# A recurrence of eight small networks on one core: the matrix passes, waits and instruction orders of all four engines rearranged

## Chip, cores and metric

The kernel runs on one core of one Trainium2 chip. The metric is the device time of one execution in microseconds (us). The kernel before took 5656.33 us, the median of three runs that lie between 5656.32 and 5656.89.

## What is computed

2048 sequences are advanced through 256 time steps. One step of one sequence, cut to what matters:

```python
encoded   = tanh(xt @ We + st @ Ue + be)                     # 24 numbers
new_state = tanh(einsum(xt, Wx) + einsum(st, Ws) + bk)       # 8 candidates of 32
inp = concatenate([encoded, err])                            # the newest of 20 remembered entries
mem = concatenate([inp, mem[:-1]])
a        = relu(mem.reshape(-1) @ enc_w1 + enc_b1)           # 500 numbers -> 64
agent_in = relu(a @ enc_w2 + enc_b2)                         # 16
h1, c1 = lstm(agent_in, h1, c1);  h2, c2 = lstm(h1, h2, c2)
gate  = softmax(h2 @ gate_w + gate_b)                        # 8
theta = clamp01(mean(abs(mem[:10, -1])) * 2.5)
gate  = gate * theta + gs * (1 - theta)
st    = sum over the 8 candidates of gate * new_state        # 32
pred  = clamp01(st[-1]);  err = pred - yt
```

Nothing of a step can be computed for good before the step ahead of it has given `st`, but for the part of `a` that comes from the 19 older entries.

## The kernel before

The sequences are split into two groups of 1024 (g = 0 and 1). One group at one step is an *item*; items are numbered n = 1, 2, ..., with the groups alternating, so item n+2 is the next step of the group of item n. There are 512 items. In what follows X is an item, Y the next one (the other group), W the one ahead of X, so the state that W leaves is what Y starts from.

Every engine executes a list of instructions written out by hand, `run_phases` (L158): once per item it calls the engine's own `phase(items, extra)` with three items in flight, `new`, `cur` and `old`, each one younger than the next. Five steps, ten phases, form one trip of a hardware loop. The engines run freely and meet only at semaphores: `wait_ge(q, n)` ahead of an instruction, `.then_inc(q, 1)` at its end. So what sets the order of the work is, on each engine, the order of the calls in `phase`, and between engines those waits. One execution of the four phase lists for one item is called a *turn* below. The length of a turn, times 512, is nearly the whole time.

**TensorE (PE), L280 to L476.** In the order of the list: `encoded_s` (L311, the state's part of the encoder input), `logit_bias` (L417) and `gate_logits` (L424) for the softmax, `encoder1_now` (L368, the newest entry's part of `a`), `encoder2` (L379), `bias_of_cell` (L390) and `cell_gates` (L402) once for each LSTM cell, `candidates_x` and `candidates_s` (L322, L338) for the eight candidate states, `encoded_x` (L300), `state_transpose` (L285). The older entries' part of `a` is `history` (L357): four blocks, each of three passes (high and low fp16 halves of weights and entries), each pass two matmuls of 512 columns that use one half of the array's columns each and run side by side. Blocks 0 and 1 of an item run a turn ahead of blocks 2 and 3. They depend on nothing recent and fill the places at which TensorE would wait.

**ScalarE (ACT), L478 to L600.** `state_take` (L495, the transposed state to SBUF), `at_least_zero` and `encoded` (L507, L500), `entry_high` (L513), `encoder1` (L520), `agent_input` (L526), `cell_tanhs` and `value_tanh` (L545, L551) of each cell, `next_hidden` (L557), the candidates' tanh in four quarters (`candidates`, L535), `exponentials` (L565).

**VectorE (DVE), L602 to L834.** `cell_terms` (L691), `cell_value` (L697) and `new_hidden` (L703) of each cell; `errors` (L682); the softmax and gate in eight small instructions (`peaks` L721, `below_peak` L726, `totals`, `reciprocals`, `shares` L742, `fresh_gate` L747, `new_gate` L753), whose result goes to PSUM; the product of candidates and gate (`mix`, L760: pair 1 whole, of pair 0 one half) and four sums over the candidates (`mix_sum`, L780, each one half hf of one pair), which give the state; `prediction` (L788).

**GpSimd (POOL), L836 to L930.** `mix_quarter` (L864, the other half of pair 0), `new_error` (L893), `keep_prediction` (L903), `kept_share` and `kept_gate` (L843, L849: the part of the gate that is kept), `entry_low` (L876, the low half of the entry) and `gate_in_sbuf` (L857). `new_gate` on VectorE waits for `kept_gate`.

**SyncE (SP), L193 to L278**, loads inputs and weights ahead and writes each entry to the ring `hist` with four DMAs once `entry_low` and `encoder1_now` of it are done; `history` of the group's next step waits for them.

The four lists before (TensorE L441, ScalarE L570, VectorE L799, GpSimd L915) are in the listing and on the removed side of the diff.

## Time and profile before

| | |
|---|---|
| median of 3 runs | 5656.33 us |
| span of the profiled execution | 5654.1 us |
| instructions | 184300 |
| TensorE busy | 5444.6 us, 96% |
| VectorE busy | 4678.1 us, 83% |
| ScalarE busy | 3830.9 us, 68% |
| GpSimd busy | 1646.7 us, 29% |
| DMA | 172.38 MB, 30 GB/s |
| mean granted TensorE clock | 0.998 of full |

A busy share counts the time in which an engine had an instruction under way. A matmul's end is modelled, so TensorE counts as busy while a matmul drains and nothing new streams. PEld is TensorE's weight load. In a timeline a row merges neighbouring instructions of one line: the first number is the start, the second the time from the first one's start to the last one's end, x how many; in brackets the engine's idle time before it and what ended it. L numbers are lines of the kernel before.

### The profile page before, as it was taken

The page shows a single profiled execution, that of the slowest core. Times are in us where ns is not written, and L with a number is a line of the kernel's source. Part 1 is how long each engine was busy: PE and PEld are TensorE (multiplying, and loading weights), DVE is VectorE, ACT ScalarE, POOL GpSimd, SP SyncE. Part 2 cuts the span into 40 slices and gives each one's busy share as a digit, 9 for nine tenths or more (in the row PEclk, how much of TensorE's full clock was granted, in tenths as well). Part 3 has the DMA queues.
Part 4 walks back from the last instruction along what each step waited for, and adds up shares of the span by engine and source line. Part 5 has one row for each costly group of instructions (what it writes and reads, how often), then busy time and mean ns, then how long its engine had stood idle before and what let it go on. Part 6 is the DMA issues. An engine that isn't in the chain of part 4 may idle for free.

```text
span 5654.1 us, 184300 instructions
## 1 busy us (share of the span) xinstructions
PE 5444.6 (96%) x67584; PEld 3397.7 (60%) x67584; DVE 4678.1 (83%) x12841; ACT 3830.9 (68%) x9217; POOL 1646.7 (29%) x3589
## 2 busy tenths in 40 slices
PE   7999999999999999999999999999999999999998
PEld 4666666666666666666666666666666666666665
DVE  7888888888888888888888888888888888888887
...
GB/s 66 28 29 30 28 31 28 31 28 31 28 31 28 31 28 28 31 28 31 28 31 28 31 28 31 28 29 30 28 31 28 31 28 31 28 31 28 31 28 39
DMA packets 299286, 172.38 MB, mean 30 GB/s; under 512 B 156734, under 2 KB 263882, under 8 KB 298714
## 3 DMA queue, kind: packets, MB, share of 16 engines
...
q14 instruction: 8, 0.07, 0.0%
...
## 4 chain that ended last, share of the span: by engine, by line
PE 69%; ACT 15%; DVE 12%; issue 4%; DMA 0%; POOL 0%; ACTq 0%; POOLq 0%; DVEq 0%
PE chain L412 17%; PE a_ps L374 10%; PE cand_ps L343 8%; PE cand_ps L334 8%; ACT a_sb L523 6%; PE chain L399 6%; PE a_ps L363 6%; ACT gates L548 5%; DVE cell_in L708 5%; DVE added L694 4%; PE chain L308 4%; PE a_ps L385 4%; PE chain L429 4%; PE cand_ps L329 3%; ACT tanh_c L554 3%
## 5 line engine op out<-in xcount | busy, mean ns | idle before, releaser
L363 PE MATMUL a_ps<-hist,w_hist 125*64 125x512 f16 x12288 | 1700.2, 381 | 24.9 <-DMA w_hist<-enc_table 24.9
L785 DVE TENSOR_REDUCE state<-mixed 128x64 f32<-128x512 f32 x2048 | 1352.6, 681 | 34.1 <-POOL mixed L873 0.7
L541 ACT ACTIVATE cand<-cand_ps 128x512 f32<-128x512 f32 x2048 | 1154.6, 590 | 184.8 <-PE cand_ps L343 184.8
L412 PE MATMUL chain<-cell_in,cell_w 128*64 128x128 f32 x16384 | 1092.8, 276 | 0.7 <-ACT cell_in L531 0.5
L412 PEld LDWEIGHTS chain<-cell_in,cell_w 128*64 128x64 f32 x16384 | 888.3, 136 | 288.2 <-ACT cell_in L531 181.5
L900 POOL TENSOR_TENSOR err_ring<-pred_now,ys 128x8 f32 x512 | 128.6, 251 | 3106.0 <-DVE pred_now L792 3106.0
L548 ACT ACTIVATE gates<-chain 128x512 f32<-128x512 f32 x1024 | 611.4, 597 | 619.8 <-PE chain L412 619.8
L363 PEld LDWEIGHTS a_ps<-hist,w_hist 125*64 125x64 f16 x12288 | 658.6, 110 | 447.2 <-issue 26.0
L554 ACT ACTIVATE tanh_c<-gates 128x128 f32<-128x128 f32 x1024 | 316.7, 309 | 690.0 <-DVE gates L700 690.0
L694 DVE SCALAR_TENSOR_TENSOR added<-gates 128x256 f32<-128x256 f32 x1024 | 435.5, 425 | 419.4 <-ACT gates L548 419.4
L708 DVE SCALAR_TENSOR_TENSOR cell_in<-gates,tanh_c 64x128 f32<-64x128 f32 x2048 | 588.0, 287 | 159.4 <-ACT tanh_c L554 145.6
L873 POOL TENSOR_TENSOR mixed<-cand,gate 128x512 f32<-128x512 f32 x512 | 653.8, 1277 | 119.3 <-POOL gate L861 119.1
L769 DVE TENSOR_TENSOR mixed<-cand,chain 128x1024 f32<-128x1024 f32 x512 | 624.9, 1220 | 17.8
L374 PE MATMUL a_ps<-entry,w_now 100*64 100x256 f32 x4096 | 555.0, 388 | 61.2 <-ACT entry L504 0.4
L334 PE MATMUL cand_ps<-w_x,x_sb 32*128 32x256 f32 x8192 | 528.6, 374 | 0.0
L343 PE MATMUL cand_ps<-w_s,state_t 32*128 32x256 f32 x8192 | 528.6, 374 | 0.0
L523 ACT ACTIVATE a_sb<-a_ps,columns 128x512 f32<-128x512 f32 x512 | 351.7, 687 | 201.8 <-PE a_ps L374 201.8
L343 PEld LDWEIGHTS cand_ps<-w_s,state_t 32*128 32x128 f32 x8192 | 401.2, 185 | 40.9
L334 PEld LDWEIGHTS cand_ps<-w_x,x_sb 32*128 32x128 f32 x8192 | 403.8, 185 | 29.3
L399 PE MATMUL chain<-indicator,cell_bias 128*64 128x512 f16 x2048 | 416.1, 403 | 0.0
L531 ACT ACTIVATE cell_in<-a_ps,columns 64x128 f32<-64x128 f32 x1024 | 371.2, 362 | 37.6 <-PE a_ps L385 0.5
L374 PEld LDWEIGHTS a_ps<-entry,w_now 100*64 100x64 f32 x4096 | 293.0, 136 | 147.9 <-issue 102.8
...
## 6 DMA issues: line engine op xcount, KB each, us to landing
...
hist<-entry_parts SPq DMA_DIRECT2D x2048, 25.0 KB
...
```

Of the source, the lines that this page charges most:

```text
L334: nc.tensor.matmul(cand_ps[q][:, NS * hf:NS * hf + NS], x_sb[rows, x_slot(u), g, P * hf:P * hf + P], w_x[rows, :], start=False, stop=False ...
L343: last = nc.tensor.matmul(cand_ps[q][:, NS * hf:NS * hf + NS], state_t[rows, g, P * hf:P * hf + P], w_s[rows, :], start=False, stop=True, ...
L363: nc.tensor.matmul(a_ps[g][ENC * half:ENC * half + ENC, :], w_hist[0:HROWS, w_slot(u), kk, wp, :], hist[0:HROWS, xp, k, at:at + 512], star ...
L374: last = nc.tensor.matmul(a_ps[g][rows, COLS * p:COLS * p + COLS], w_now[0:ER, p, rows], entry[0:ER, g, :], start=False, stop=True, skip_g ...
L399: nc.tensor.matmul(chain[g][rows, :], cell_bias[:, c, rows], indicator[:, :], start=True, stop=False, skip_group_check=True)
L412: last = nc.tensor.matmul(chain[g][rows, P * r:P * r + P], cell_w[c][:, hf, r, :], cell_in[c][:, g, hf, :], start=False, stop=True, skip_g ...
L523: nc.scalar.activation(a_sb[:, g, :], a_ps[g][:, :], ACT.Relu, bias=enc1_bias[:, 0:1])\
L541: ins = nc.scalar.activation(cand[:, g, q // 2, :, q % 2, :, :].rearrange("p h s c -> p h (s c)"), cand_ps[q][:, :].rearrange("p (h k) -> ...
L548: nc.scalar.activation(gates[c][:, g, 0:4, :].rearrange("p r b -> p (r b)"), chain[g][:, :], ACT.Tanh).then_inc(q_gates[c], 1)
L694: V.scalar_tensor_tensor(added[c][:, g, :, :], gates[c][:, g, 1:3, :], 1.0, gates[c][:, g, 3:5, :], ALU.add, ALU.mult).then_inc(q_added[c], 1)
L708: last = V.scalar_tensor_tensor(cell_in[1][rows, g, hf, :], gates[c][rows, g, 0, :], 1.0, tanh_c[c][rows, g, :], ALU.add, ALU.mult)
L785: V.tensor_reduce(state[:, g, hf, 2 * pair:2 * pair + 2, :], mixed[:, pair, hf, :, :, :], AX, ALU.add)\
```

## The change

No arithmetic instruction is added or removed, and none changes its shape or operands. Changed are orders and waits:

- `history` can issue single passes; the twelve passes of an item are spread over six places instead of in four blocks. The order on TensorE is new: `encoded_x` comes after `cell_gates` of cell 1, the candidates' matmuls after one history pass.
- `q_sum[hf]`, one semaphore for the two sums of a half, becomes one semaphore per sum. `state_transpose` and `prediction` wait for each; `prediction` has four waits in place of two.
- The waits of `candidates` on ScalarE are split by quarter; the waits of `encoder1_now` and `entry_high` change places; the wait for the row of `y` (in `errors`) becomes a call of its own ahead of `thetas`; some waits that others imply are dropped.
- The sums: before, the order of an item was (hf 1, pair 0), (0, 0), (0, 1), (1, 1), the cell-0 terms of the next item after the first; now it is (1, 1), (0, 1), then all of cell 0 of the next item, then (1, 0), (0, 0).
- `prediction` moves from between `cell_value` and `new_hidden` of cell 1 to behind `below_peak`; `thetas` moves ahead of `new_hidden` of cell 1.
- ScalarE: `exponentials` moves ahead of `entry_high`, candidate quarter 3 leaves its place after `encoded`, quarter 1 goes behind `agent_input`, `next_hidden` behind the tanh of cell 0.
- GpSimd: `mix_quarter` runs at the end of its own item's phase and no longer at the head of the next, `new_error` right behind it, `keep_prediction` one phase later.

The diff, cut to its core (initial counts of semaphores, signatures and the splitting of `agent_input`, `next_hidden` and `new_hidden` by half, whose instructions stay together, are left out):

```diff
 TENSOR_HEAD = 0
-SUMS = 2
 ENTRY_ROWS = (slice(0, HALF), slice(HALF, ER))
 HIST_INC = 16 * Q
-CAND_ORDER = (2, 1, 3, 0)
-MIX_ORDER = (1, 0)
+CAND_ORDER = (3, 2, 0, 1)
+FIRST_HALF = (0, 0)
+PIECES = ((0, 0), (1, 0), (0, 1))
 assert 1 + LOOPS * PER_TILE == STEPS and HT * PER_TILE == MEM
...
             def state_transpose(item, hf):
                 g, n, u = item
-                pe.wait_ge(q_sum[hf], SUMS * n)
+                for pair in range(2):
...
-            def candidates_x(item, before, extra):
-                g, n, u = item
-                if before:
-                    for q in CAND_ORDER:
-                        pe.wait_ge(q_cand[q], before[1])
+            def candidates_bias(item):
+                g, n, u = item
+                for q in CAND_ORDER:
+                    pe.wait_ge(q_cand[q], n)
                 for q in range(Q):
...
-            def history(item, kk):
+
+            def history(item, kk, first=0, end=len(PIECES)):
                 g, n, u = item
                 k = HT - 1 - kk
-                for t, (wp, xp) in enumerate(((0, 0), (1, 0), (0, 1))):
+                for t in range(first, end):
...
             def encoder1_now(item):
                 g, n, u = item
+                pe.wait_ge(q_err, n)
                 pe.wait_ge(q_enc, n)
-                pe.wait_ge(q_err, n)
...
             def phase(items, extra):
                 new, cur, old = items
                 if cur:
+                    history(cur, 1, 2, 3)
+                    history(cur, 2, 0, 1)
+                if old:
+                    cell_gates(old, 0)
+                if cur:
+                    history(cur, 2, 1, 2)
+                if old:
+                    candidates_bias(old)
+                    candidates_x(old)
+                    candidates_s(old)
+                    bias_of_cell(old, 1)
+                    cell_gates(old, 1)
+                if cur:
+                    encoded_x(cur, extra)
+                    state_transpose(cur, 0)
+                    state_transpose(cur, 1)
+                    history(cur, 2, 2, 3)
+                if new:
+                    history_waits(new, extra)
+                    history(new, 0, 0, 1)
+                if cur:
                     encoded_s(cur)
+                if new:
+                    history(new, 0, 1, 2)
+                if cur:
+                    history(cur, 3, 0, 2)
                 if old:
                     logit_bias(old)
-                if cur:
-                    history(cur, 3)
-                if old:
                     gate_logits(old)
                 if cur:
+                    history(cur, 3, 2, 3)
                     encoder1_now(cur)
                 if new:
-                    history_waits(new, old, extra)
-                    history(new, 0)
+                    history(new, 0, 2, 3)
+                    history(new, 1, 0, 1)
                 if cur:
                     encoder2(cur)
                     bias_of_cell(cur, 0)
                 if new:
-                    history(new, 1)
-                if cur:
-                    cell_gates(cur, 0)
-                    candidates_x(cur, old, extra)
-                    candidates_s(cur)
-                    bias_of_cell(cur, 1)
-                if new:
-                    encoded_x(new, old, extra)
-                if cur:
-                    cell_gates(cur, 1)
-                if new:
-                    state_transpose(new, 0)
-                    state_transpose(new, 1)
-                    history(new, 2)
-
...
             def candidates(item, q):
                 g, n, u = item
                 if q == CAND_ORDER[0]:
                     act.wait_ge(q_candps, n)
-                    act.wait_ge(q_mul[MIX_ORDER[1]], n)
-                    act.wait_ge(q_mulpool, n)
+                if q // 2 == 1:
+                    act.wait_ge(q_mul[1], n)
+                elif q == 0:
+                    act.wait_ge(q_mul[0], n)
+                else:
+                    act.wait_ge(q_mulpool[1], n)
                 ins = nc.scalar.activation(cand[:, g, q // 2, :, q % 2, :, :].rearrange("p h s c -> p h (s c)"),
                                            cand_ps[q][:, :].rearrange("p (h k) -> p h k", h=HF), ACT.Tanh)
                 ins.then_inc(q_cand[q], 1)
...
             def phase(items, extra):
                 new, cur, old = items
-                if cur:
-                    agent_input(cur)
-                if old:
-                    next_hidden(old)
-                if cur:
-                    cell_tanhs(cur, 0)
-                    value_tanh(cur, 0)
-                    candidates(cur, 2)
-                    candidates(cur, 1)
-                    cell_tanhs(cur, 1)
                 if new:
                     state_take(new)
                 if cur:
                     at_least_zero(new)
                     encoded(new)
                 if cur:
-                    candidates(cur, 3)
+                    exponentials(cur)
                 if new:
                     entry_high(new)
-                if cur:
-                    exponentials(cur)
-                if new:
                     encoder1(new)
                 if cur:
                     candidates(cur, 0)
+                if new:
+                    agent_input(new, 0)
+                    agent_input(new, 1)
+                if cur:
+                    candidates(cur, 1)
+                if new:
+                    cell_tanhs(new, 0)
+                if cur:
+                    next_hidden(cur, 0)
+                    next_hidden(cur, 1)
+                if new:
+                    value_tanh(new, 0)
+                    candidates(new, 3)
+                    candidates(new, 2)
+                    cell_tanhs(new, 1)
...
+            def error_rows_wait(item, extra):
+                g, n, u = item
                 if g == 0:
                     dve.wait_ge(s_y[x_slot(u)], extra[0][u] if u >= 0 else 16)
+
+            def errors(item):
...
             def mix_sum(item, hf, pair):
                 g, n, u = item
-                dve.wait_ge(q_mul[pair], n + GROUPS if pair == MIX_ORDER[1] else n)
+                dve.wait_ge(q_mul[pair], n + GROUPS)
                 if pair == 0:
-                    dve.wait_ge(q_mulpool, n + GROUPS)
+                    dve.wait_ge(q_mulpool[1], n + GROUPS)
                 V.tensor_reduce(state[:, g, hf, 2 * pair:2 * pair + 2, :], mixed[:, pair, hf, :, :, :], AX, ALU.add)\
-                    .then_inc(q_sum[hf], 1)
+                    .then_inc(q_sum[hf][pair], 1)
 
             def prediction(item):
                 g, n, u = item
                 for hf in range(HF):
-                    dve.wait_ge(q_sum[hf], SUMS * n + SUMS * GROUPS)
+                    for pair in range(2):
+                        dve.wait_ge(q_sum[hf][pair], n + GROUPS)
                 V.tensor_scalar(pred_now[:, g, :].rearrange("p (a h l) -> p a h l", a=2, h=HF),
                                 state[:, g, :, :, S - 1].rearrange("p h (a l) -> p a h l", a=2),
                                 1.0, 0.0, ALU.min, ALU.max).then_inc(q_pred, 1)
...
             def phase(items, extra):
                 new, cur, old = items
-                if cur:
-                    new_hidden(cur, 0)
                 if old:
                     mix_sum(old, 0, 1)
-                    mix_sum(old, 1, 1)
+                if cur:
+                    cell_terms(cur, 0)
+                    cell_value(cur, 0)
+                    new_hidden(cur, 0, 0)
+                    new_hidden(cur, 0, 1)
+                if old:
+                    mix_sum(old, 1, 0)
+                    mix_sum(old, 0, 0)
                 if cur:
                     error_sum(cur)
                     cell_terms(cur, 1)
                     cell_value(cur, 1)
+                if new:
+                    error_rows_wait(new, extra)
+                if cur:
+                    thetas(cur)
+                    new_hidden(cur, 1, 0)
+                    new_hidden(cur, 1, 1)
+                if new:
+                    errors(new)
+                if cur:
+                    peaks(cur)
+                    below_peak(cur)
                 if old:
                     prediction(old)
                 if cur:
-                    new_hidden(cur, 1)
-                if new:
-                    errors(new, extra)
-                if cur:
-                    thetas(cur)
-                    peaks(cur)
-                    below_peak(cur)
                     totals(cur)
                     reciprocals(cur)
...
                     new_gate(cur)
                     mix(cur, 1)
                     mix(cur, 0)
-                    mix_sum(cur, 1, 0)
-                if new:
-                    cell_terms(new, 0)
-                    cell_value(new, 0)
-                if cur:
-                    mix_sum(cur, 0, 0)
+                    mix_sum(cur, 1, 1)
 
...
-            def mix_quarter(item):
+            def mix_quarter(item, q):
                 g, n, u = item
                 pool.wait_ge(q_keptfrom, n + GROUPS)
-                pool.wait_ge(q_cand[1], n)
+                pool.wait_ge(q_cand[q], n + 1)
 
                 for hf in range(HF):
-                    pool.wait_ge(q_sum[hf], SUMS * n + SUMS * (GROUPS - 1))
-                over_s = gate[:, g, 1:Q:2, :].rearrange("p h (o c) -> p h o c", o=1)\
+                    pool.wait_ge(q_sum[hf][0], n + (GROUPS - 1))
+                over_s = gate[:, g, q:Q:2, :].rearrange("p h (o c) -> p h o c", o=1)\
                     .to_broadcast([P, HF, S, C])
-                G.tensor_tensor(mixed[:, 0, :, 1, :, :], cand[:, g, 0, :, 1, :, :], over_s, ALU.mult)\
-                    .then_inc(q_mulpool, 1)
+                G.tensor_tensor(mixed[:, 0, :, q, :, :], cand[:, g, 0, :, q, :, :], over_s, ALU.mult)\
+                    .then_inc(q_mulpool[q], 1)
 
...
                 step, ring = place(item, extra)
+                pool.wait_ge(q_pred, n)
                 pred = pred_now[:, g, :].rearrange("p (j o) -> p j o", o=1)
                 G.tensor_copy(preds[:, tiles, bass.ds(step, 1)], pred).then_inc(q_predout, 1)
...
             def phase(items, extra):
                 new, cur, old = items
-                if old:
-                    mix_quarter(old)
-                    new_error(old, extra)
-                    keep_prediction(old, extra)
                 if cur:
                     kept_share(cur)
                     kept_gate(cur)
                     entry_low(new)
                 if cur:
                     gate_in_sbuf(cur)
+                    mix_quarter(cur, 1)
+                    new_error(cur, extra)
+                if old:
+                    keep_prediction(old, extra)
 
             run_phases(pool, phase, turn_start)
 ```

## Rows read from the trace of the kernel before

**Rows 1.** The page: the chain of work that ended last, by engine

```profile
PE 69%; ACT 15%; DVE 12%; issue 4%; DMA 0%; POOL 0%; ACTq 0%; POOLq 0%; DVEq 0%
```

**Rows 2.** One line's instructions (L374): duration in ns min/median/max, first and last start in us

```profile
L374 PE MATMUL a_ps<-entry,w_now x4096: 378/379/431, 32.3 to 5625.2; 100*64 100x256 f32 x196
```

**Rows 3.** Timeline of TensorE over one turn, from 2808.86 us: start, length, idle before

```profile
2808.86 0.59 PE L288 MATMUL chain<-ident,state 128*128 128x128 f32 x2
...
2810.05 0.60 PE L315 MATMUL chain<-state_t,w_ue 128*64 128x256 f32 x4
...
2810.52 0.82 PE L363 MATMUL a_ps<-hist,w_hist 125*64 125x512 f16 x6
2811.39 0.43 PE L429 MATMUL chain<-gate_w,cell_in 128*64 128x32 f32 x8
2811.93 1.08 PE L374 MATMUL a_ps<-entry,w_now 100*64 100x256 f32 x8
...
2815.08 1.09 PE L412 MATMUL chain<-cell_in,cell_w 128*64 128x128 f32 x16
...
2818.83 1.04 PE L412 MATMUL chain<-cell_in,cell_w 128*64 128x128 f32 x16
2819.80 0.59 PE L288 MATMUL chain<-ident,state 128*128 128x128 f32 x2
```

**Rows 4.** Timeline of VectorE, same turn

```profile
2809.62 0.43 DVE L694 SCALAR_TENSOR_TENSOR added<-gates 128x256 f32<-128x256 f32 x1 [0.41 <-ACT gates L548]
...
2810.29 0.17 DVE L792 TENSOR_SCALAR pred_now<-state 128x8 f32<-128x8 f32 x1
2810.74 0.59 DVE L708 SCALAR_TENSOR_TENSOR cell_in<-gates,tanh_c 64x128 f32<-64x128 f32 x2 [0.29 <-ACT tanh_c L554]
2811.36 0.42 DVE L687 SCALAR_TENSOR_TENSOR entry<-clamped,y_rows 4x256 f32<-4x256 f32 x1
...
2812.14 0.22 DVE L729 TENSOR_TENSOR logit<-chain,peak 128x64 f32<-128x64 f32 x1
...
2813.18 0.17 DVE L745 TENSOR_TENSOR share<-recip,theta 128x8 f32<-128x8 f32 x1
...
2813.64 0.23 DVE L757 TENSOR_TENSOR chain<-fresh,kept 128x64 f32<-128x64 f32 x1
...
2815.05 0.68 DVE L777 TENSOR_TENSOR mixed<-cand,chain 128x512 f32<-128x512 f32 x1
...
2816.85 0.42 DVE L694 SCALAR_TENSOR_TENSOR added<-gates 128x256 f32<-128x256 f32 x1 [0.40 <-ACT gates L548]
...
2818.72 1.28 DVE L785 TENSOR_REDUCE state<-mixed 128x64 f32<-128x512 f32 x2
```

**Rows 5.** Timeline of ScalarE, same turn

```profile
2809.49 0.38 ACT L498 ACTIVATE state_t<-chain 128x256 f32<-128x256 f32 x1
...
2811.14 0.47 ACT L504 ACTIVATE entry<-chain,columns 96x256 f32<-96x256 f32 x1
```

**Rows 6.** Timeline of GpSimd, same turn

```profile
2810.67 0.21 POOL L900 TENSOR_TENSOR err_ring<-pred_now,ys 128x8 f32 x1 [6.05 <-DVE pred_now L792]
...
2812.07 0.20 POOL L846 TENSOR_TENSOR one_theta<-ones,theta 128x8 f32<-128x8 f32 x1 [0.97 <-DVE theta L679]
2812.35 0.30 POOL L853 TENSOR_TENSOR kept<-gate,one_theta 128x64 f32<-128x64 f32 x1
2812.60 0.67 POOL L879 TENSOR_TENSOR entry_parts<-entry,entry_parts 128x256 f16<-128x256 f32 x1
```

**Rows 7.** L708 and L900 five turns later (two timelines); L900's group on the page

```profile
2865.41 0.63 DVE L708 SCALAR_TENSOR_TENSOR cell_in<-gates,tanh_c 64x128 f32<-64x128 f32 x2 [0.20 <-ACT tanh_c L554]
...
2865.43 0.34 POOL L900 TENSOR_TENSOR err_ring<-pred_now,ys 128x8 f32 x1 [6.14 <-DVE pred_now L792]
...
L900 POOL TENSOR_TENSOR err_ring<-pred_now,ys 128x8 f32 x512 | 128.6, 251 | 3106.0 <-DVE pred_now L792 3106.0
```

**Rows 8.** Timeline: SyncE issuing the four DMAs of one entry, same turn

```profile
2813.40 3.69 SPq L267 DMA_DIRECT2D hist<-entry_parts  x4
```

86 lines of the change are left out of this document (46 added, 40 removed).

## Prediction

> **What bounds the kernel now.** I read the chain of waits first: 69% of it is work on TensorE, the rest is mostly what TensorE waits for on ScalarE (15%) and VectorE (12%) [rows 1]. Then one line's first and last start, for the length of a turn: `encoder1_now` runs once a turn, first at 32.3 us, the last of its eight matmuls at 5625.2 and that one 0.70 after the call's first (1.08 less the 0.38 of one) [rows 2, 3]. (5592.9 - 0.7)/511 = 10.943 us a turn; 511 turns are 5592 of the 5654.1 us of the span, the rest is loading and draining. So the question is what one turn costs, and 0.01 us a turn is 5 us. The median of the runs lies 2.2 us above the span; I add that at the end. About 0.2% (11 us, 0.022 us a turn) is what a measurement of this kernel can tell from no change.
>
> Then the timelines of the engines over one turn. From one transpose to the next are 10.94 us [rows 3]. No engine is full: TensorE drains and waits between the LSTM cells' matmuls and the instructions that need them. The turn is a loop of dependences through all engines, and the new length is that of the longest loop under the new order. I time two loops; W, X, Y are items as above.
>
> **Loop A: through the state and the gate.** I start it at `cell_terms` of cell 0 of X.
> - `cell_terms` to the end of `new_hidden`: 1.71 (2809.62 to 2810.74 + 0.59, cell 1, where nothing stood between) [rows 4]. Before, a sum stood ahead of cell 0's `new_hidden`; the change takes it away. `next_hidden`, moved here, falls in ScalarE's wait for `cell_value`.
> - To the first matmul of `cell_gates` 1: 0.06 (2811.33 to 2811.39, the same hop at `gate_logits`). `cell_gates` up to the transpose, the shape switch included: 0.97 (2818.83 to 2819.80), and 0.05 for a first pass whose weights wait (1.09 against 1.04). `encoded_x` now stands between the two: 0.44, as `encoded_s` of equal shape, whose start to the next history pass is 0.47 with the tiny `logit_bias` [rows 3]. Together 1.46. The `encoded_x` that left the front of `cell_gates` 1 buys only the wait that VectorE allows there.
> - Transposes to `encoded_s`: 0.63 + 0.38 + 0.05 = 1.06 [rows 3, 5]. Two history passes fill it (0.22 each: six matmuls, three pairs, take 0.82, the last 0.38 of it [rows 3]).
> - `encoded_s`, `logit_bias` and three single passes: 0.47 + 0.66 = 1.13. `new_hidden` 1 is done by then.
> - `gate_logits` to `below_peak`: 0.70, 0.05 less than from 2811.39 to 2812.14, since `thetas` no longer stands ahead of `peaks` [rows 3, 4].
>
> So `below_peak` starts 6.12 after the loop's start; call that moment L. VectorE needs 1.50 from L to `new_gate` (2812.14 to 2813.64), then 1.41 to the second product (2815.05), and 0.60 each for it and the two sums that now stand ahead of the next item's `cell_terms` (two sums take 1.28, one of them 0.68, so they start 0.60 apart) [rows 4]: 3.21. Sum: 6.12 + 1.50 + 3.21 = **10.83**.
>
> **Loop B: without the gate.** `cell_gates` 0 to `cell_terms` 1.77 (2815.08 to 2816.85) [rows 3, 4]; then 1.71 + 0.06 + 1.46 + 1.06 = 4.29 to `encoded_s` as above; then to `encoder1_now` 1.66: 1.04 to `encoded` (1.09 less 0.05 of waiting), 0.47 for it, and 0.15 as from the end of `errors` (2811.78) to 2811.93 [rows 3, 4, 5]; then 3.15 to the next `cell_gates` 0 (2811.93 to 2815.08), where three single passes in place of a block of three cost nothing. Sum: **10.87**. Single passes cost nothing elsewhere either: every one lies in a wait of a loop.
>
> By these two sums alone the turn falls by 0.07, 37 us in all.
>
> **What the change adds: GpSimd between two instructions of VectorE.** Before, the prediction of W ran ahead of `new_hidden` 1, and GpSimd was through with `new_error` and `keep_prediction` when `theta` came. Now `prediction` of W stands behind `below_peak` of X, and on GpSimd `kept_share` and `kept_gate` of X are queued behind `new_error` of W, which waits for it. Behind them is `entry_low` of Y, and `new_gate` of X waits for `kept_gate`. From L: the prediction starts 0.14 later and takes 0.17; `new_error` follows 0.21 after its end (2810.46 to 2810.67) [rows 4, 6], at L + 0.52; then 0.15 and 0.13 until `kept_share` (estimates from a 0.21 long instruction and one of 0.19, each overlapped 0.06), 0.28 to `kept_gate`, at L + 1.08, 0.30 for it, and `entry_low` starts 0.25 after it, at L + 1.33, and takes 0.67, until L + 2.00 [rows 6]. `kept_gate` is done at L + 1.38, in time for `new_gate` at L + 1.50. But `entry_low` now runs right through the start of `new_gate`. Before, it was over 0.37 ahead of it (2813.27 against 2813.64) [rows 4, 6].
>
> Does that matter? Rows 7 against rows 4 and 6. In the usual turn `new_error` starts 0.07 ahead of `new_hidden` and takes 0.21; the pair of `new_hidden` takes 0.59. Five turns later `new_hidden` starts 0.02 first: `new_error` takes 0.34, and the pair 0.63. Each holds up the other. All turns of `new_error` have a mean of 251 ns [rows 7]; with 0.21 and 0.34 that is some 30% slow ones, and 0.3 x 0.04 is the 0.012 by which the mean turn exceeds 10.93. So both instructions, which read two SBUF operands, don't run beside a GpSimd instruction that reads SBUF. `new_gate` reads `fresh` and `kept`, `entry_low` reads two operands for most of 0.67 us.
>
> The price isn't shown before. From below: `share`, also of two operands, started 0.09 ahead of `entry_low`'s end and took its normal 0.17 [rows 4, 6], so the hold ends 0.14 or so ahead of the end: `new_gate` would start at L + 1.86, 0.36 late. From above: the second `new_hidden` of rows 7 finished 0.27 after `new_error`'s end, its usual length (0.29), so nothing of it was done before: L + 2.01, 0.51 late. I take 0.41, nearer the row with `entry_low` itself. Loop A becomes 10.83 + 0.41 = **11.24**: (11.24 - 10.943) x 511 = 152 us more, 5805.9 on the span, 5808 for the median. Its own range is 0.36 to 0.51, 5780 to 5862.
>
> The Trainium skill ("SBUF — State Buffer", section "SBUF: two separate sides") calls the port pair of VectorE and GpSimd an exclusive lock: an instruction with two SBUF inputs and a GpSimd one that reads SBUF exclude each other, and the later blocks until the other is over. The trace agrees that both are delayed; by the rule to the letter `new_gate` would wait until L + 2.03, and the turn be 11.36.
>
> **Other parts.** The earlier `thetas` and wait for `y`, split semaphores and changed order of waits lie beside other work. `mix_quarter` (nothing waits for it until the sums behind cell 0, over 3 us later) and `entry_high` behind `exponentials` have cover. The history passes that are drawn ahead of `encoded_s` need the entry of X in memory: its four DMAs are issued over 3.7 us [rows 8], and there are some 7 us from `entry_low` to that pass now (about 10 before). Cover is there unless a landing takes over 3 us.
>
> **Rivals.**
> 1. *No hold on `new_gate`* (chance 0.16): a hold as in rows 7, 0.04, or none. Loop A is 10.83 to 10.87, loop B decides: 10.87, 5617 on the span, **5619**, faster by 0.7%. For it: a hold this long is nowhere in the trace, and `share` was not held. Against: `share` came when `entry_low` was all but over.
> 2. *The gain is eaten by waits* (0.10): the hold is absent, but the four waits of `prediction`, of which three are instructions of their own, delay GpSimd's queue by about 0.07 and loop A or B comes out at 10.94: **5656**, no change.
> 3. *A part of the hold* (0.09): GpSimd gives way in the middle of `entry_low`, 0.15 to 0.35 late: 10.98 to 11.18, 5677 to 5780.
> 4. *Worse* (0.05): GpSimd's queue is later by 0.1 and the hold whole, or the history DMAs land late: above 5870.
>
> The forecast, 0.60, rests on rows that show both directions of the exclusion. The range of 8 in 10 takes in the forecast's own 5780 to 5862 and, below it, rivals 3 and 2: 5640 to 5870. Faster by over 0.2% is rival 1 (0.16), within 0.2% rival 2 (0.10), slower the rest (0.74).
>
> **What would show it.** In the timeline after, `new_gate` (the small VectorE instruction that writes `chain` from `fresh` and `kept`) takes some 0.6 in place of 0.23, or starts late, and ends with `entry_low`; `kept_gate` ends about 0.1 ahead of its start; the two candidates' sums stand right ahead of `cell_terms`. TensorE then waits longer ahead of `cell_gates` 1, and its waits no longer fall on `encoder1_now`. The forecast is wrong if `new_gate` keeps 0.23 us beside a running `entry_low`, or if `entry_low` starts after it. A turn of 10.87 with ScalarE's `a_sb` ending the waits would be loop B.

## The result, and the profile after

The changed kernel takes 5791.25 us (median of 4 runs, 5790.65 to 5791.59), the kernel before 5656.56 (4 runs, 5656.32 to 5656.89): a ratio of 1.0238, 95% interval 1.0224 to 1.0253. It is slower, by 135 us. The profiled execution has a span of 5788.8 us (before 5654.1), with a mean granted clock of 0.998 of full speed (2.4 GHz).

The page, share of the span by engine and the chain that ended last (compare [rows 1]):

```profile
PE 5424.3 (94%) x67584; PEld 3313.1 (57%) x67584; DVE 4858.4 (84%) x12848; ACT 3872.6 (67%) x9217; POOL 1541.3 (27%) x3589
...
DVE 40%; PE 35%; issue 16%; ACT 5%; POOL 2%; DVEq 1%; POOLq 1%; DMA 0%; ACTq 0%
```

The chain that ended last went through TensorE for 69% before; now VectorE holds more of it than TensorE. `encoder1_now` gives the length of a turn, as in [rows 2]:

```profile
L375 PE MATMUL a_ps<-entry,w_now x4096: 379/379/430, 31.9 to 5758.5; 100*64 100x256 f32 x196
```

(5758.5 - 31.9 - 0.7) / 511 = 11.205 us a turn, against 10.943. The usual turn has 11.14 (some 355 of 510); nearly all others lie between 11.30 and 11.42. TensorE over one usual turn (start, length, idle before), to set beside [rows 3]:

```profile
2809.91 0.42 PE L430 MATMUL chain<-gate_w,cell_in 128*64 128x32 f32 x8
2810.16 0.39 PE L364 MATMUL a_ps<-hist,w_hist 125*64 125x512 f16 x2
2810.46 1.08 PE L375 MATMUL a_ps<-entry,w_now 100*64 100x256 f32 x8
...
2813.60 1.09 PE L413 MATMUL chain<-cell_in,cell_w 128*64 128x128 f32 x16
...
2817.51 1.09 PE L413 MATMUL chain<-cell_in,cell_w 128*64 128x128 f32 x16 [0.20 <-DVE cell_in L732]
2818.43 0.60 PE L308 MATMUL chain<-x_sb,w_we 128*36 128x256 f32 x4
2818.96 0.44 PE L290 MATMUL chain<-ident,state 128*128 128x128 f32 x2
...
2819.87 0.65 PE L315 MATMUL chain<-state_t,w_ue 128*64 128x256 f32 x4
...
2821.04 0.43 PE L430 MATMUL chain<-gate_w,cell_in 128*64 128x32 f32 x8
```

The wait of TensorE now stands ahead of `cell_gates` of cell 1 and is ended by VectorE's `cell_in`. VectorE in the same turn ([rows 4]):

```profile
2810.64 0.23 DVE L754 TENSOR_TENSOR logit<-chain,peak 128x64 f32<-128x64 f32 x1
2810.82 0.17 DVE L817 TENSOR_SCALAR pred_now<-state 128x8 f32<-128x8 f32 x1
...
2811.88 0.27 DVE L775 TENSOR_TENSOR fresh<-expd,share 128x64 f32<-128x64 f32 x1
2812.19 0.60 DVE L782 TENSOR_TENSOR chain<-fresh,kept 128x64 f32<-128x64 f32 x1
2812.82 1.22 DVE L793 TENSOR_TENSOR mixed<-cand,chain 128x1024 f32<-128x1024 f32 x1
2813.96 0.68 DVE L801 TENSOR_TENSOR mixed<-cand,chain 128x512 f32<-128x512 f32 x1
2814.56 1.27 DVE L809 TENSOR_REDUCE state<-mixed 128x64 f32<-128x512 f32 x2
2815.75 0.41 DVE L718 SCALAR_TENSOR_TENSOR added<-gates 128x256 f32<-128x256 f32 x1
...
2816.86 0.59 DVE L732 SCALAR_TENSOR_TENSOR cell_in<-gates,tanh_c 64x128 f32<-64x128 f32 x2 [0.38 <-ACT tanh_c L569]
...
2820.40 0.58 DVE L732 SCALAR_TENSOR_TENSOR cell_in<-gates,tanh_c 64x128 f32<-64x128 f32 x2 [0.29 <-ACT tanh_c L569]
```

And GpSimd ([rows 6]):

```profile
2811.20 0.21 POOL L929 TENSOR_TENSOR err_ring<-pred_now,ys 128x8 f32 x1 [6.91 <-DVE pred_now L817]
...
2811.78 0.29 POOL L882 TENSOR_TENSOR kept<-gate,one_theta 128x64 f32<-128x64 f32 x1
2812.03 0.67 POOL L908 TENSOR_TENSOR entry_parts<-entry,entry_parts 128x256 f16<-128x256 f32 x1
```

`new_gate` (L782) takes 0.60 in place of 0.23 and ends at 2812.79, with `entry_low` (L908), which ends at 2812.70. `kept_gate` (L882) ends 0.12 ahead of `new_gate`'s start. From `new_gate` to `cell_terms` (L718) VectorE no longer waits: the 0.40 of idle time ahead of L694 in [rows 4] is gone. `cell_terms` comes 3.56 after `new_gate`'s start, and TensorE waits for what follows it. `gate_logits` too (2821.04) comes right behind VectorE, 0.06 after the end of `new_hidden` 1 (2820.40 + 0.58).

`new_gate` over the whole run (duration in ns min/median/max; then who ended VectorE's idle time before it, us and times):

```profile
L782 DVE TENSOR_TENSOR chain<-fresh,kept x512: 232/605/620, 44.7 to 5772.5; 128x64 f32<-128x64 f32 x171
...
  POOL kept L882: 43.5, 152
```

Those 152 are the long turns (GpSimd's `kept` comes late there). One of them, VectorE and GpSimd:

```profile
2832.91 0.22 DVE L754 TENSOR_TENSOR logit<-chain,peak 128x64 f32<-128x64 f32 x1
...
2834.63 0.62 DVE L782 TENSOR_TENSOR chain<-fresh,kept 128x64 f32<-128x64 f32 x1 [0.26 <-POOL kept L882]
...
2833.57 0.21 POOL L929 TENSOR_TENSOR err_ring<-pred_now,ys 128x8 f32 x1 [7.00 <-DVE pred_now L817]
...
2834.15 0.38 POOL L882 TENSOR_TENSOR kept<-gate,one_theta 128x64 f32<-128x64 f32 x1
2834.49 0.67 POOL L908 TENSOR_TENSOR entry_parts<-entry,entry_parts 128x256 f16<-128x256 f32 x1
```

`new_error` (L929) starts 0.66 after L754 instead of 0.56, `kept_gate` then starts together with `fresh` and takes 0.38, and `new_gate` starts 1.72 after L754 instead of 1.55. That is 0.17 more for the gate, and 0.16 to 0.28 for the long turns. The long turns are not scattered: they are the same three of every ten, and ten turns are one trip of the hardware loop. At two places of the trip `new_error` starts 0.31 to 0.32 after the end of the prediction, at the other eight 0.21; at a third `new_error` is on time and `kept_share` behind it is 0.27 late. At these three places `new_gate` starts 1.72, 1.74 and 1.81 after L754. In the kernel before, too, `new_error` is 0.10 late at two places of ten.

### The profile page after: what moved, and what is told of

It reads as the page before. It is cut to its first block, busy times and chain, and to the rows that moved or that the text cites. A ratio compares the mean times of both kernels' runs of the same rounds, so it can differ in the third digit from the quotient of the medians.

```text
span 5788.8 us, 184676 instructions
## 1 busy us (share of the span) xinstructions
PE 5424.3 (94%) x67584; PEld 3313.1 (57%) x67584; DVE 4858.4 (84%) x12848; ACT 3872.6 (67%) x9217; POOL 1541.3 (27%) x3589
## 4 chain that ended last, share of the span: by engine, by line
DVE 40%; PE 35%; issue 16%; ACT 5%; POOL 2%; DVEq 1%; POOLq 1%; DMA 0%; ACTq 0%
PE a_ps L364 11%; DVE state L809 10%; PE chain L413 10%; DVE mixed L801 6%; DVE chain L782 5%; PE chain L315 5%; PE chain L308 4%; PE chain L290 3%; DVE added L718 3%; DVE cell_in L732 3%; ACT tanh_c L569 3%; DVE gates L724 3%; PE chain L430 3%; DVE peak L749 2%; DVE fresh L775 2%
## 5 line engine op out<-in xcount | busy, mean ns | idle before, releaser
L364 PE MATMUL a_ps<-hist,w_hist 125*64 125x512 f16 x12288 | 1887.7, 382 | 24.1 <-DMA w_hist<-enc_table 24.1
L809 DVE TENSOR_REDUCE state<-mixed 128x64 f32<-128x512 f32 x2048 | 1305.9, 679 | 15.7
L413 PE MATMUL chain<-cell_in,cell_w 128*64 128x128 f32 x16384 | 1119.9, 279 | 139.3 <-DVE cell_in L732 138.8
L413 PEld LDWEIGHTS chain<-cell_in,cell_w 128*64 128x64 f32 x16384 | 873.6, 136 | 468.2 <-DVE cell_in L732 290.2
L929 POOL TENSOR_TENSOR err_ring<-pred_now,ys 128x8 f32 (+1 forms) x512 | 108.8, 212 | 3578.9 <-DVE pred_now L817 3578.9
L364 PEld LDWEIGHTS a_ps<-hist,w_hist 125*64 125x64 f16 x12288 | 709.2, 110 | 405.9 <-issue 128.8
L732 DVE SCALAR_TENSOR_TENSOR cell_in<-gates,tanh_c 64x128 f32<-64x128 f32 x2048 | 586.2, 286 | 356.5 <-ACT tanh_c L569 342.7
L569 ACT ACTIVATE tanh_c<-gates 128x128 f32<-128x128 f32 x1024 | 316.6, 309 | 503.8 <-DVE gates L724 503.8
L793 DVE TENSOR_TENSOR mixed<-cand,chain 128x1024 f32<-128x1024 f32 x512 | 625.1, 1221 | 17.6
L718 DVE SCALAR_TENSOR_TENSOR added<-gates 128x256 f32<-128x256 f32 x1024 | 429.9, 420 | 197.4 <-ACT gates L563 197.4
L375 PE MATMUL a_ps<-entry,w_now 100*64 100x256 f32 x4096 | 555.0, 388 | 0.2 <-DVE entry L711 0.2
L386 PE MATMUL a_ps<-a_sb,w_enc 128*32 128x128 f32 x4096 | 218.1, 285 | 176.7 <-ACT a_sb L533 176.7
```

Source lines behind the costliest of these rows:

```text
L364: nc.tensor.matmul(a_ps[g][ENC * half:ENC * half + ENC, :], w_hist[0:HROWS, w_slot(u), kk, wp, :], hist[0:HROWS, xp, k, at:at + 512], star ...
L375: last = nc.tensor.matmul(a_ps[g][rows, COLS * p:COLS * p + COLS], w_now[0:ER, p, rows], entry[0:ER, g, :], start=False, stop=True, skip_g ...
L413: last = nc.tensor.matmul(chain[g][rows, P * r:P * r + P], cell_w[c][:, hf, r, :], cell_in[c][:, g, hf, :], start=False, stop=True, skip_g ...
L718: V.scalar_tensor_tensor(added[c][:, g, :, :], gates[c][:, g, 1:3, :], 1.0, gates[c][:, g, 3:5, :], ALU.add, ALU.mult).then_inc(q_added[c], 1)
L732: last = V.scalar_tensor_tensor(cell_in[1][rows, g, hf, :], gates[c][rows, g, 0, :], 1.0, tanh_c[c][rows, g, :], ALU.add, ALU.mult)
L793: V.tensor_tensor(mixed[:, 1, :, :, :, :].rearrange("p h l s c -> p (h l) s c"), cand[:, g, 1, :, :, :, :].rearrange("p h l s c -> p (h l) ...
```

## Experiments

Each run is compared with the kernel before on the same chip (medians 5657.48, 5656.91 and 5656.01 in the three groups of runs). To read them all in one way I cut the turn into four stretches between starts on TensorE: a, `cell_gates` 0 to `cell_gates` 1; b, on to `gate_logits`; c, on to `encoder1_now`; d, on to the next `cell_gates` 0. They are medians over 300 turns of each profiled execution, and say where the time lies, not which wait sets it. The last columns are the usual turn, the mean turn and the time.

```
kernel                       a     b     c     d     turn   mean    us
before                       3.75  3.49  0.55  3.15  10.93  10.944  5656.6
after                        3.91  3.54  0.55  3.15  11.14  11.204  5791.3
low_last                     3.54  3.54  0.54  3.14  10.77  10.831  5604.8
prediction_early             3.88  3.54  0.54  3.15  11.12  11.123  5749.6
gate_one_operand             3.55  3.54  0.54  3.14  10.78  10.839  5606.2
low_writes_only              3.55  3.54  0.55  3.15  10.78  10.840  5604.6
before_prediction_late       3.75  3.49  0.55  3.15  10.93  10.947  5658.9
low_last_prediction_early    3.54  3.54  0.54  3.15  10.77  10.769  5568.6
low_last_blocks              3.54  3.61  0.55  3.14  10.85  10.900  5635.6
low_last_x_first             3.97  3.49  0.48  3.14  11.07  11.069  5722.3
sum_in_wait                  3.67  3.54  0.54  3.15  10.89  10.899  5635.3
best_sum_in_wait             3.67  3.54  0.54  3.15  10.89  10.895  5632.7
before_x_behind              3.67  3.61  0.51  3.15  10.93  10.952  5660.3
```

### low_last: entry_low behind gate_in_sbuf

The theory: the hold costs more than the whole loss. The rival: the new orders on TensorE or the waits make the turn longer.

```diff
                 if cur:
                     kept_gate(cur)
+                if cur:
+                    gate_in_sbuf(cur)
                 if new:
                     entry_low(new)
                 if cur:
-                    gate_in_sbuf(cur)
                     mix_quarter(cur, 1)
```

> The changed kernel with entry_low moved behind gate_in_sbuf on GpSimd, nothing else. Theory (new_gate on VectorE can't run beside entry_low, both read SBUF operands over one shared path): new_gate falls from 0.60 to 0.23 us, the usual turn from 11.14 to 10.77 (loop B could set it at up to 10.87), the three turns in ten whose kept_gate is late to about 10.95; mean 10.82, so some 5595 us, at most 5640. Rival (it is GpSimd's queue behind prediction that costs the time, new_gate merely looks long): kept_gate comes no sooner, so the time stays above 5770.

5604.76 us, ratio 0.9907 (0.9891 to 0.9924). VectorE and GpSimd:

```profile
2807.34 0.23 DVE L782 TENSOR_TENSOR chain<-fresh,kept 128x64 f32<-128x64 f32 x1
...
2807.38 0.36 POOL L890 TENSOR_TENSOR gate<-fresh,kept 128x64 f32<-128x64 f32 x1 [0.16 <-DVE fresh L775]
2807.70 0.67 POOL L908 TENSOR_TENSOR entry_parts<-entry,entry_parts 128x256 f16<-128x256 f32 x1
```

With `entry_low` out of the way `new_gate` takes 0.23 again and stretch a falls from 3.91 to 3.54. Without the hold, the rest of the change is on balance 53 us faster than the kernel before; the hold costs 186 us.

### prediction_early: the prediction back ahead of new_hidden 1

```diff
                 if new:
                     error_rows_wait(new, extra)
+                if old:
+                    prediction(old)
                 if cur:
                     thetas(cur)
...
                     below_peak(cur)
-                if old:
-                    prediction(old)
-                if cur:
                     totals(cur)
```

> The changed kernel with prediction put back ahead of new_hidden of cell 1 on VectorE, GpSimd's list unchanged. kept_gate is then done over a microsecond early, and entry_low waits for entry_high alone and starts at once behind it, some 0.7 ahead of new_gate's start: it should meet share and fresh_gate, which also read two SBUF operands, in place of new_gate. Theory (hold): share or fresh_gate is held until about 0.14 ahead of entry_low's end, new_gate is its usual 0.23 and ends about 0.1 earlier than now; no late turns any more; turn about 11.03, some 5700 us. Rival (the queue behind prediction is the cost): all of the loss goes, turn about 10.8, 5590 us.

5749.57 us, 1.0163 (1.0146 to 1.018). This expectation was too low by 50 us, but on the side of the hold: `new_gate` was to end 0.1 earlier than in the changed kernel, and ends 0.03 earlier (2.12 after the start of L754, not 2.15), since `fresh` and `new_gate` both still follow behind the held instruction.

```profile
2803.34 0.55 DVE L770 TENSOR_TENSOR share<-recip,theta 128x8 f32<-128x8 f32 x1
2803.93 0.23 DVE L775 TENSOR_TENSOR fresh<-expd,share 128x64 f32<-128x64 f32 x1
2804.19 0.23 DVE L782 TENSOR_TENSOR chain<-fresh,kept 128x64 f32<-128x64 f32 x1
...
2803.20 0.67 POOL L907 TENSOR_TENSOR entry_parts<-entry,entry_parts 128x256 f16<-128x256 f32 x1 [1.08 <-ACT entry_parts L527]
```

`entry_low` starts earlier now and strikes `share` (L770): 0.55 for 0.17 (551 ns is its mean over all turns). The hold is not bound to one instruction. It strikes whichever one of two SBUF operands comes while `entry_low` runs. The turns with a late `kept_gate` are gone; that is most of what this kernel gains on the changed one. The hold of `share` is worth 181 us: low_last_prediction_early (below) differs from this kernel by `entry_low`'s place alone and takes 5568.59.

### gate_one_operand and low_writes_only: two ways to end the hold, no order changed

```diff
-                V.tensor_tensor(fresh[:, g, :, :], expd[:, g, :, :], over_c(share, g), ALU.mult)\
+                V.tensor_tensor(fresh_ps(g), expd[:, g, :, :], over_c(share, g), ALU.mult)\
...
-                V.tensor_tensor(gate_ps(g), fresh[:, g, :, :], kept[:, g, :, :], ALU.add)\
+                V.tensor_tensor(gate_ps(g), fresh_ps(g), kept[:, g, :, :], ALU.add)\
...
+                    fresh_in_sbuf(cur)
                     mix(cur, 1)
```

`fresh` is written to PSUM, so `new_gate` reads one operand from SBUF; `fresh_in_sbuf` copies it for GpSimd.

> The changed kernel, but fresh is written to PSUM, new_gate reads it there (so it has one SBUF operand, kept), and a copy from PSUM to SBUF for GpSimd is added right behind new_gate. Theory (hold needs two SBUF operands): new_gate takes about 0.23 beside a running entry_low; the copy adds 0.26 to the loop; usual turn 11.14 - 0.37 + 0.26 = 11.03, mean 11.08, about 5725 us. Rival (any VectorE instruction that touches SBUF is held by entry_low): new_gate stays at 0.6 and the added copy comes on top, turn 11.4, 5890 us.

5606.17 us, 0.991 (0.9893 to 0.9926):

```profile
2809.57 0.23 DVE L791 TENSOR_TENSOR chain<-chain,kept 128x64 f32<-128x64 f32 x1
2809.71 0.21 DVE L785 COPY fresh<-chain 128x64 f32<-128x64 f32 x1
2809.84 1.22 DVE L802 TENSOR_TENSOR mixed<-cand,chain 128x1024 f32<-128x1024 f32 x1
...
2809.40 0.67 POOL L918 TENSOR_TENSOR entry_parts<-entry,entry_parts 128x256 f16<-128x256 f32 x1
```

The same instruction beside the same running `entry_low` takes 0.23 when one of its operands lies in PSUM. The expected time was 120 us too high: the added copy costs nothing, since it fits between `new_gate` and the first product, which starts 0.27 after `new_gate` with or without it.

The second edit leaves VectorE alone and turns `entry_low` into one column and two memsets (it leaves out the low half of 255 columns of the entry).

```diff
-                G.tensor_tensor(entry_parts[:, g, 1, :], entry[:, g, :], entry_parts[:, g, 0, :],
-                                ALU.subtract).then_inc(q_el, 1)
+                G.tensor_tensor(entry_parts[:, g, 1, 0:1], entry[:, g, 0:1], entry_parts[:, g, 0, 0:1],
+                                ALU.subtract)
+                G.memset(spare[:, g, :], 0.0)
+                G.memset(entry_parts[:, g, 1, 1:COLS], 0.0).then_inc(q_el, 1)
```

> The changed kernel, but entry_low's subtraction is done for one column only; two memsets (one of a spare tile, one of the rest of the low half) take its place, so GpSimd is busy for a similar time there and only writes. This leaves out the low half of the entries' fp16 split. Theory (the hold is for GpSimd instructions that read SBUF): new_gate 0.23 to 0.3, mean turn 10.8 to 10.9, 5590 to 5640 us. Rival (any GpSimd instruction holds VectorE's two-operand ones): new_gate 0.5 or more, time above 5740.

5604.63 us, 0.9906 (0.989 to 0.9923):

```profile
2809.86 0.23 DVE L783 TENSOR_TENSOR chain<-fresh,kept 128x64 f32<-128x64 f32 x1
...
2809.82 0.31 POOL L911 MEMSET spare<- 128x256 f32 x1
2810.07 0.31 POOL L912 MEMSET entry_parts<- 128x255 f16 x1
```

`new_gate`, again of two SBUF operands, isn't held by GpSimd instructions that only write. So it takes both: two operands read from SBUF on VectorE and reading on GpSimd.

### before_prediction_late: the same hold in the kernel before

```diff
-                if old:
-                    prediction(old)
                 if cur:
                     new_hidden(cur, 1)
...
                     below_peak(cur)
+                if old:
+                    prediction(old)
+                if cur:
                     totals(cur)
```

> The kernel before, with prediction alone moved behind below_peak on VectorE. Theory: GpSimd's queue then puts entry_low beside new_gate here too and new_gate takes some 0.6 us, but here VectorE stands idle 0.40 ahead of cell_terms, which takes the 0.37, and the turn is set by a loop over TensorE without the gate; the 0.04 that new_error and new_hidden cost each other in three turns of ten goes away. So 5650 to 5675 us with a new_gate of 0.6. Rival (a held new_gate always costs its length, or the late queue does): 5657 + 511 x 0.37 = 5846 us.

5658.93 us, 1.0003 (0.9994 to 1.0012):

```profile
2803.98 0.60 DVE L757 TENSOR_TENSOR chain<-fresh,kept 128x64 f32<-128x64 f32 x1
...
2807.13 0.43 DVE L694 SCALAR_TENSOR_TENSOR added<-gates 128x256 f32<-128x256 f32 x1
```

`new_gate` takes 0.60 here too, and the kernel is not slower. The idle time ahead of `cell_terms` (L694), 0.40 in [rows 4], has vanished: the hold was paid out of it. A hold by itself is not a loss.

### sum_in_wait and best_sum_in_wait: where one sum stands

If a wait of VectorE can pay for the hold, giving it back in the changed kernel should do the same. Before, one sum stood between `cell_value` and `new_hidden` of cell 0. Both kernels put one there again, the first into the changed kernel, the second into low_last_prediction_early (below).

```diff
-                if old:
-                    mix_sum(old, 0, 1)
                 if cur:
                     cell_terms(cur, 0)
                     cell_value(cur, 0)
+                if old:
+                    mix_sum(old, 0, 1)
+                if cur:
                     new_hidden(cur, 0, 0)
```

> The changed kernel, with one of the two sums that stand ahead of cell_terms of cell 0 put back between cell_value and new_hidden, where VectorE waits for ScalarE. The hold of new_gate stays as it is. Theory: the hold of 0.37 us counts only because VectorE no longer waits between new_gate and cell_terms. With the sum moved, new_gate still takes 0.60, but VectorE waits again ahead of cell_terms, which then starts 1.77 after cell_gates of cell 0; new_hidden ends 1.84 later (1.71 and 0.13 for the sum, as in the kernel before), cell_gates 1 follows at 3.67 instead of 3.91, and the other three stretches of TensorE keep 3.54, 0.54 and 3.15: turn 10.90, about 5635 us, at most 5660. Rival: the hold costs the turn its whole length wherever the sums stand: new_hidden 0 comes no earlier, 5790 us or more (one sum more in its way: up to 5850).

5635.29 us, 0.9963 (0.995 to 0.9977):

```profile
2802.96 0.60 DVE L782 TENSOR_TENSOR chain<-fresh,kept 128x64 f32<-128x64 f32 x1
...
2806.14 0.42 DVE L718 SCALAR_TENSOR_TENSOR added<-gates 128x256 f32<-128x256 f32 x1
2806.60 0.29 DVE L724 SCALAR_TENSOR_TENSOR gates<-added 128x128 f32<-128x128 f32 x1
2806.81 0.68 DVE L809 TENSOR_REDUCE state<-mixed 128x64 f32<-128x512 f32 x1
2807.41 0.57 DVE L732 SCALAR_TENSOR_TENSOR cell_in<-gates,tanh_c 64x128 f32<-64x128 f32 x2
```

The hold is still there in full, and the kernel is 156 us faster than the changed one, by one moved sum.

> The same sum put back, in the version without a hold (entry_low behind gate_in_sbuf, prediction ahead of new_hidden of cell 1; 5568.6 us). Theory: without the hold the free place of the sum costs: new_hidden of cell 0 ends 0.13 later than its gates allow, cell_gates 0 to cell_gates 1 is 3.67 in place of 3.54, turn 10.90, about 5635 us. So the sum's new place is worth 0.13 us a turn without the hold, and lays VectorE open to it with the hold. Rival: cell_gates 1 waits for TensorE's own work (3.54) and 0.13 of new_hidden is hidden: no change, 5569 us.

5632.72 us, 0.9958 (0.9945 to 0.9972). Without a hold the same place of the sum costs 64 us, 0.13 us a turn in stretch a. With it and without it the time is nearly the same, 5635 and 5633: in that order the hold is hidden.

### low_last_prediction_early: both harmless

`entry_low` behind `gate_in_sbuf`, and the prediction ahead of `thetas`; the two diffs above together.

> The changed kernel with entry_low behind gate_in_sbuf and prediction ahead of new_hidden of cell 1: nothing of GpSimd's lies beside share, fresh_gate and new_gate, and kept_gate is early. Theory: the usual turn stays at 10.77, set by a loop over TensorE (cell_gates 0 to cell_gates 1 3.53, to gate_logits 3.54, to encoder1_now 0.54, to the next cell_gates 0 3.15 = 10.76), and the three late turns in ten (0.18 to 0.26 longer in low_last) vanish: mean 10.77, 5573 us. Rival (the late turns come from elsewhere, register work or the loop's edge): 5600 us.

5568.59 us, 0.9843 (0.9829 to 0.9856): the fastest of all, 88 us under the kernel before. The long turns, still there in low_last, are gone, since `kept_gate` is done 1.7 us ahead of `new_gate`:

```profile
2799.87 0.46 POOL L881 TENSOR_TENSOR kept<-gate,one_theta 128x64 f32<-128x64 f32 x1
...
2802.01 0.23 DVE L782 TENSOR_TENSOR chain<-fresh,kept 128x64 f32<-128x64 f32 x1
```

The usual turn is that of low_last, 10.77, though `new_gate` comes 0.05 sooner: it is no longer set by the gate. What sets it is read from the waits along the way from `cell_gates` 1 to `encoder1_now` (stretches b and c together). `encoder1_now` waits for two things, `encoded` on ScalarE, which comes through the transposes and `encoded_s`, and `errors` on VectorE, which stands behind `new_hidden` 1. Medians over the same 300 turns (the last three kernels are described below):

```
kernel                       cell_gates 1   transposes    encoded_s    from the end of      new_hidden 1   sum
                             to transposes  to encoded_s  to encoded's encoded  errors      to             b + c
                                                          end          to encoder1_now      gate_logits
before                       0.97           1.19          1.56         0.33     0.15        0.06           4.04
after                        1.46           0.91          1.57         0.15     0.15        0.06           4.08
low_last                     1.46           0.91          1.57         0.14     0.15        0.06           4.08
low_last_prediction_early    1.46           0.91          1.57         0.14     0.14        0.06           4.08
low_last_blocks              1.46           1.04          1.52         0.14     0.19        0.13           4.16
low_last_x_first             0.97           1.05          1.70         0.25     0.08        0.06           3.97
before_x_behind              1.46           1.04          1.52         0.10     0.15        0.13           4.12
```

In the first four kernels with the changed order of waits (after to low_last_blocks) `encoder1_now` keeps 0.14 to 0.15 behind `encoded`, while its distance from `errors` moves up to 0.19; and `errors` can be followed in 0.08 (low_last_x_first). So there the way through transposes, `encoded_s` and `encoded` sets it, which is the prediction's loop B: 3.54 + 4.08 + 3.15 = 10.77. Stretch a, 3.54, is the data's way through cell 0: `cell_gates` 1 starts 0.05 after the end of `new_hidden` 0, the shortest such gap in any of the kernels.

### low_last_blocks, low_last_x_first, before_x_behind: the order on TensorE

The first is low_last with each item's twelve history passes in four blocks again:

```diff
-                if cur:
-                    history(cur, 1, 2, 3)
-                    history(cur, 2, 0, 1)
...
                     state_transpose(cur, 1)
-                    history(cur, 2, 2, 3)
-                if new:
-                    history_waits(new, extra)
-                    history(new, 0, 0, 1)
-                if cur:
+                    history(cur, 2)
                     encoded_s(cur)
-                if new:
-                    history(new, 0, 1, 2)
-                if cur:
-                    history(cur, 3, 0, 2)
+                    history(cur, 3)
```

> low_last with history issued in whole blocks of three passes again (block 2 ahead of encoded_s, 3 behind it, 0 behind encoder1_now, 1 behind bias_of_cell), the rest of TensorE's new order kept. By sums from low_last's timeline: transposes to encoded_s 1.02 in place of 0.91, encoder1_now 0.11 later, so usual turn 10.88, about 5640 to 5655 us. Rival (where a pass stands is indifferent, they fill waits either way): 5605 us.

5635.59 us, 0.9963 (0.9949 to 0.9976), a little under the range: the single passes are worth 31 us. The usual turn is 0.08 longer, and the place is the expected one: three history passes ahead of `encoded_s` instead of two make transposes to `encoded_s` 1.04 instead of 0.91, of which 0.05 comes back behind `encoded_s`, and `encoder1_now` keeps its 0.14 behind `encoded`. The table shows the time in stretch b because `gate_logits` is late as well, 0.13 behind `new_hidden` 1 instead of 0.06, but nothing on the longest way waits for that.

The second is low_last with `encoded_x` ahead of `cell_gates` 1, as before:

```diff
                     bias_of_cell(old, 1)
-                    cell_gates(old, 1)
                 if cur:
                     encoded_x(cur, extra)
+                if old:
+                    cell_gates(old, 1)
+                if cur:
                     state_transpose(cur, 0)
```

> low_last with encoded_x ahead of cell_gates of cell 1 again, as before the change. Theory (the usual turn is a loop through TensorE's order: cell_gates 0, cell_gates 1, gate_logits, encoder1_now): TensorE reaches cell_gates 1 0.43 later and nothing is gained behind it, since gate_logits waits for new_hidden of cell 1: turn up to 11.19, about 5815 us. Rival (as the prediction had it, the loop through transposes, encoded_s and encoder1_now sets the turn, in which encoded_x counts the same on either side): 5605 us.

5722.33 us, 1.0115 (1.0099 to 1.013): the direction of the theory, but 93 us less than it expected. Stretch a is longer by 0.43, all of `encoded_x` (0.44 on TensorE): without it TensorE's own work fills that stretch to some 3.53 (an estimate, 3.97 less 0.44), so it has nothing to hide `encoded_x` in. b and c are shorter by 0.12 together; no more is gained there because `encoder1_now` then follows `errors`, which waits for `new_hidden` 1 (0.08 in the table above).

```profile
2806.80 0.60 PE L308 MATMUL chain<-x_sb,w_we 128*64 128x256 f32 x4
2807.24 1.04 PE L413 MATMUL chain<-cell_in,cell_w 128*64 128x128 f32 x16
2808.36 0.44 PE L290 MATMUL chain<-ident,state 128*128 128x128 f32 x2
```

So the move is worth 118 us in this order: 0.30 on the usual turn, 0.24 on the mean one, since this kernel has none of low_last's long turns. The run doesn't speak against loop B in low_last: `encoded_x` counts the same on either side only while TensorE has idle time ahead of `cell_gates` 1, and here it has none. The third kernel is the one before with this move alone:

```diff
-                if new:
-                    encoded_x(new, old, extra)
                 if cur:
                     cell_gates(cur, 1)
                 if new:
+                    encoded_x(new, old, extra)
                     state_transpose(new, 0)
```

> The kernel before, with only encoded_x moved behind cell_gates of cell 1. Theory: the move pays only together with the single history passes and the sums' order. cell_gates 0 to cell_gates 1 falls from 3.75 to 3.67 alone, since new_hidden of cell 0 ends there (the sum ahead of it), and cell_gates 1 to gate_logits grows from 3.49 to 3.61, since two history passes more than fit stand ahead of gate_logits (as in the run with whole blocks): turn 10.97, about 5670 us. Rival: the move is worth by itself what it is worth in the changed kernel, 0.30 us a turn: about 5505 us; or 0.08, the TensorE wait alone, without the loss: 5617 us.

5660.3 us, 1.0007 (0.9998 to 1.0016):

```profile
2810.04 1.09 PE L412 MATMUL chain<-cell_in,cell_w 128*64 128x128 f32 x16 [0.18 <-DVE cell_in L707]
2810.97 0.60 PE L308 MATMUL chain<-x_sb,w_we 128*36 128x256 f32 x4
```

By itself the move gives nothing: stretch a falls by 0.08, only to 3.67, where TensorE waits for the `new_hidden` that the sum holds back, and from `cell_gates` 1 to `encoder1_now` it is 0.09 more (4.12 for 4.04), since `encoded_x` now stands ahead of the transposes and blocks of three passes ahead of `encoded_s`. It pays together with the sum's new place (a can fall to 3.54) and the single passes (b and c together 4.08).

## Why the prediction was right, and where it was not

The forecast was 5808 with its own range of 5780 to 5862, by a hold of 0.36 to 0.51 on `new_gate`. 5791 lies in it, and the named mechanism is the one that the runs show.

**The hold: right, 0.04 too long.** Predicted 0.41, measured 0.37 (0.60 less 0.23). The lower bound, 0.36, was nearly the measured one: `new_gate` ends 0.09 after `entry_low`, so 0.14 of its 0.23 lie before that end, and of `share`'s 0.17 in prediction_early 0.15 do. But the row it rests on (`share` unheld 0.09 ahead of `entry_low`'s end) gives at least 0.09; that it would be 0.14 was not in it, and its coming out was luck. The upper bound doesn't follow from its row either: an end 0.27 after `entry_low`'s, less the 0.23 of `new_gate`, is L + 2.04, 0.54 late, not 0.51. And by the prediction's own sums 0.36 and 0.51 give 5782 and 5859, not 5780 and 5862. To the letter, the rule of the Trainium skill ("SBUF — State Buffer", section "SBUF: two separate sides") would have the loser blocked until the other is over; the runs with one PSUM operand (0.23) and with memsets (0.23) agree with its conditions, and the 0.14 and 0.15 say that `new_gate` and `share` get there sooner than a start behind the profiled end would allow.

**GpSimd's timetable: right within 0.06.** Counted from L, the start of L754: `new_error` 0.56 (predicted 0.52; the prediction starts 0.18 after L, not 0.14), `kept_gate` 1.14 (1.08), `entry_low` 1.39 to 2.06 (1.33 to 2.00). `kept_gate`, running now beside `fresh`, made that 0.27 for 0.22, so `new_gate` starts at L + 1.55, not 1.50.

**Loop A, step by step.** `cell_terms` to the end of `new_hidden` 1.70 (1.71); to `cell_gates` 1 0.06 (0.06); to the transposes 1.45 (1.46); to `encoded_s` 0.91 (1.06); to `gate_logits` 1.17 (1.13); to L 0.73 (0.70); to `new_gate` 1.55 (1.50); to the second product 1.77 (1.41 + 0.41); to `cell_terms` 1.79 (1.80). Sum 11.13 for 11.24. The largest miss is "Transposes to `encoded_s`: 0.63 + 0.38 + 0.05". The 0.63 was read as the transposes' own time and held a wait: before, the second one starts 0.06 after the end of VectorE's last sum, turn after turn (2818.72 + 1.28 = 2820.00 in [rows 4]; the pair of 2819.80 in [rows 3] ends with a matmul of 0.33, which starts at 2820.06). In the changed kernel it starts 0.37 after that sum, and the pair takes 0.44 instead of 0.59; in low_last_x_first it takes 0.44 right behind `cell_gates` as well. Because of the miss a sentence next to it is wrong too, "`new_hidden` 1 is done by then": `gate_logits` comes 0.06 after `new_hidden` 1's end and waits for it, so from `cell_gates` 1 to `gate_logits` loop A goes through cell 1 on ScalarE and VectorE (3.54), not through TensorE's passes (3.65 by the forecast's sum).

**The long turns: not foreseen in the sum.** The forecast counted one turn for all. In 152 of them GpSimd's queue is late (by 0.10 in the one shown) and the turn 0.16 to 0.28 longer, 0.065 on the mean, 33 us. That is what rival 4 describes, for the same three turns in every ten. It hid the 0.10 by which the usual turn was estimated too long: 11.24 against a mean of 11.205 looks better than its parts. That the prediction's late place makes them is shown (low_last has them, low_last_prediction_early has not); their fixed places in the loop's trip rule out a cause that drifts or is random, but what GpSimd does at those places is open.

**The turn without a hold: the right loop, 0.10 too long.** The forecast had 10.87, set by loop B; low_last has 10.77. In low_last_prediction_early, where the gate is out of the way, loop B does set the turn, and its terms are off in the same place as loop A's: transposes to `encoded_s` 0.91 for 1.06, and `encoded_s` to `encoder1_now` 1.72 for 1.66 (0.15 too long, 0.06 too short). The other terms hold within 0.01. So rival 1's 5619 was 14 us too high for low_last, and 50 for the version without long turns. The expectations of low_last_prediction_early and low_last_x_first, which put this turn down to TensorE's own order, name the right four stretches but not what ends the waits in them.

**"The `encoded_x` that left the front of `cell_gates` 1 buys only the wait that VectorE allows": true, but not priced.** For the kernel before it holds (a 3.75 to 3.67, given back behind `cell_gates` 1). But the moved sum, which I booked under another step, widens what VectorE allows by 0.13, and with the single passes the move is worth 0.30 on low_last's usual turn.

**"Single passes cost nothing": right; they also save 0.08 on the usual turn** between the transposes and `encoded_s`, which the text did not count.

**What the sum's move does: missed.** The forecast took the sum's new place as a plain gain of loop A. It also spent VectorE's wait ahead of `cell_terms`, the reserve that would have paid for a hold. With one sum behind `cell_value` as before, the whole change would have been faster than before, 5635 us, hold and all.
